# Token stages of a two-block metaformer: centring and variance as 64x64 tiles, hidden banks read in pairs

## The chip, the cores and the metric

The kernel runs on one core of one Trainium2 chip. The metric is the device time of one execution in microseconds (us). The core has the matmul engine (TensorE, PE in the profile), VectorE (DVE), ScalarE (ACT), GpSimd (POOL) and SyncE (SP), which issues the DMAs. Each of them works through its own queue in order and waits on semaphores.

## The reference, cut to what matters

The input is four images of 48 channels and 128x128 pixels in float32. Two blocks follow each other, each of a convolution part and a feed-forward part on tokens, where a token is the 48 channels of one pixel:

```
def _ln_t(v, eps=1e-05):
    m = jnp.mean(v, axis=-1, keepdims=True)
    s = jnp.var(v, axis=-1, keepdims=True)
    return (v - m) / jnp.sqrt(s + eps)
x = x + _L0_conv_ref(_ln_c(x), ...)
t = _to_tokens(x)
t = t + _L0_ffn_ref(_ln_t(t), L0_ffn_W1, L0_ffn_b1, L0_ffn_W2, L0_ffn_b2)
x = _from_tokens(t, x)
x = x + _L1_conv_ref(_ln_c(x), ...)
t = _to_tokens(x)
t = t + _L1_ffn_ref(_ln_t(t), ...)
```

A feed-forward part is a normalisation over the 48 channels, a linear layer to 192 hidden values, a bias and a ReLU, and a linear layer back to 48, with values rounded to an 8-bit float before each product and to a 16-bit float after it. `_ln_c` is the same normalisation ahead of a convolution part.

## The kernel before, in words

The program is a row of stages with a barrier between them: `expand`, `gated_conv`, `token_mix` for the first block, `wavelet`, `attention_maps`, `fusion`, and `token_mix` for the second block. The change is in `token_mix` (lines 669 to 1060) alone. It runs twice. I call the runs the first and the second token stage.

A step of a token stage handles 512 pixels of two images at once: image h (0 or 1) lies on partitions 64h to 64h+47. There are 64 steps (32 blocks of pixels, two pairs of images). The pieces of a step's work are:

- `project` (lines 852, 855 in the first stage, 858 in the second): a linear layer of the convolution part; VectorE adds the residual (`add_residual`, lines 1006, 1008, 1011), which gives `x1`.
- `centre_in` (L863): a matmul with a 112x112 matrix that holds `I - 1/48` for each image's 48 channels, so it subtracts the mean. ScalarE squares the result (L926), `variance` (L881) averages the squares by a second 112x112 matmul, ScalarE takes `Ln` (L933) and `Exp` (L936) for the reciprocal root, and VectorE multiplies (`quantize_norm`, L1019), which gives the 8-bit `xq`.
- `hide(m)` (L894), m = 0, 1: two matmuls, one for each image, 96 hidden values each. ScalarE rounds each of the four results to 16 bits (`round_hidden(m)`, L943, which reads one bank of 512 columns at a time), VectorE adds bias and ReLU for each m (L1025) and casts all to 8 bits (`quantize_hidden`, L1033).
- `show` (L906): four matmuls that sum into `x2_bank`; ScalarE rounds (`round_shown`, L949), VectorE adds bias and residual (`add_shown`, L1039, L1044), and the result `x2` is stored.
- In the first stage alone, a second normalisation of `x2` for the following convolution: `centre_out` (L869), a square (L926), `variance("out")` (L881), `Ln` and `Exp`, `normalise` (L1053), and a store.

PSUM has eight banks. The first stage uses four for centring, two for `x1_bank` (projection and variance of `x1`) and `x2_bank` (`show` and variance of `x2`), and two for the hidden values. So there `hide(1)` writes over the banks of `hide(0)` and waits for ScalarE's copies (`h16_ready`). The second stage has four hidden banks and no such wait.

The order on each engine is written out by a list of pairs (stage, piece), which `staged` walks: in turn k, a piece with stage s works on step k - s. In the first stage PE's list is

```
pieces = [(0, project), (3, show), (2, hide(0)), (4, centre_out), (2, hide(1)), (1, variance("in")), (5, variance("out")), (0, centre_in)]
```

and ScalarE's list is

```
pieces = [(3, round_shown), (2, round_hidden(0)), (4, square("out")), (2, round_hidden(1)), (1, root("in")), (5, root("out")), (0, square("in"))]
```

VectorE's list is `add_residual`, `add_shown`, `bias_hidden`, `quantize_hidden`, `quantize_norm`, `normalise`. `project` waits until `Ln` of step k-2 has read `x1_bank`. `show` waits for `hq` (L1033) and, in the first stage, for `Ln` of the variance that shares `x2_bank` with it.

## Time and profile before

| | |
|---|---|
| runs, median of 3 | 2696.87 us (2694.13 to 2699.63) |
| profiled execution, its own time | 2706.45 us |
| span of its trace | 2704.7 us |
| TensorE busy | 2289.2 us (85%) |
| VectorE busy | 1528.8 us (57%) |
| ScalarE busy | 1125.6 us (42%) |
| granted TensorE clock, mean | 0.923 of full |

The span runs from the first to the last instruction; the execution's own time is 1.75 us longer. A matmul in float32 stands in the trace as two records, so 64 centrings of a stage are x128. The length of a record holds a tail after its last column, so records that follow each other without a gap overlap. PEclk is the granted TensorE clock: 1.00 is 2.4 GHz and 0.50 is 1.2 GHz, the only two levels in this trace.

### The profile page before, as it was taken

How to read it: one execution, taken by the hardware profiler on the slowest of the kernel's cores; microseconds unless marked ns; L12 is line 12 of the kernel's file. 1: busy time of each engine (PE TensorE's matmuls, PEld its weight loads, DVE VectorE, ACT ScalarE, POOL GpSimd, SP SyncE). 2: the span in 40 equal slices, each digit the busy share in tenths (PEclk: the TensorE clock that was granted, in tenths of full speed). 3: DMA queues.
4: the chain of work that ended last, by engine and by line, in shares of the span. 5: the costliest groups of instructions: out<-in, count | busy, mean ns of one | idle time of the engine just before them, and what ended most of it. 6: DMA issues, size and time to landing. Idle time of an engine off the chain costs nothing. (4 is left out here: it accounts for less than half of the span.)

```text
span 2704.7 us, 62201 instructions
## 1 busy us (share of the span) xinstructions
PE 2289.2 (85%) x21290; PEld 1246.6 (46%) x21290; DVE 1528.8 (57%) x2692; ACT 1125.6 (42%) x2338; POOL 443.6 (16%) x677
## 2 busy tenths in 40 slices
PE   5677749859998799999869999999975999688887
PEld 2334325647776333333336676666651232233332
DVE  3344421101112577777658888888861455477776
ACT  4344412101111688888723222322210121477776
POOL 7510001510000000000024444444420000000000
PEclk9888857979999899999969999999986899799998
DMA  6987875987773677777556666666636999233332
GB/s 137 260 226 213 230 217 188 311 252 277 272 274 133 125 145 145 150 144 144 109 110 149 149 139 140 146 149 144 138 100 128 237 266 255 76 105 105 105 105 76
DMA packets 533431, 457.77 MB, mean 169 GB/s; under 512 B 316712, under 2 KB 445680, under 8 KB 529970
## 3 DMA queue, kind: packets, MB, share of 16 engines
q1 hardware_dynamic: 462738, 424.85, 61.8%
q0 software_dynamic: 6032, 23.54, 3.4%
q10 hardware_dynamic: 64560, 7.92, 2.2%
q8 instruction: 78, 1.28, 0.2%
q14 instruction: 23, 0.19, 0.0%
HBM read 271.56 MB, written 186.40 MB: 169 GB/s over the span
## 5 line engine op out<-in xcount | busy, mean ns | idle before, releaser
L593 PE MATMUL gate_ps<-gate_data,gate_wt 64*64 64x289 f32 x6144 | 392.1, 412 | 48.3 <-DVE gate_out L654 29.3
L593 PEld LDWEIGHTS gate_ps<-gate_data,gate_wt 64*64 64x64 f32 x6144 | 296.7, 135 | 144.8 <-issue 64.4
L654 DVE TENSOR_TENSOR gate_out<-gate_gelu,gate_ps 128x578 f32<-128x578 f32 x96 | 72.2, 756 | 413.9 <-PE gate_ps L593 342.8
L943 ACT CAST mix_h<-mix_bank 96x512 f16<-96x512 f32 x512 | 267.6, 593 | 6.3 <-PE mix_bank L894 2.5
L1600 POOL TENSOR_TENSOR wav_diag<-wav_eye,wav_coefs 128x256 f32<-128x256 f32 x96 | 77.4, 827 | 885.8 <-DVE wav_up_cols L1680 816.3
L631 ACT ACTIVATE gate_gelu<-gate_ps 128x578 f32<-128x578 f32 x96 | 62.7, 653 | 372.0 <-PE gate_ps L593 321.8
L2020 PE MATMUL fus_bank<-fus_xt,fus_taps 76*32 76x512 f32 x1344 | 164.0, 641 | 29.0 <-DMA fus_shift<-gate_shift 24.6
L286 DVE COPY exp_out<-exp_y 128x384 f32<-128x384 f32 x192 | 102.8, 567 | 150.6 <-PE exp_y L249 148.9
L1025 DVE TENSOR_SCALAR mix_hb<-mix_h,mix_b1q 96x1024 f16<-96x1024 f16 x256 | 122.7, 479 | 93.6 <-ACT mix_h L943 93.6
L894 PE MATMUL mix_bank<-mix_xq,mix_w1q 112*96 112x512 fp8e5 x512 | 143.5, 382 | 29.1 <-ACT mix_h L943 23.0
L1033 DVE CAST mix_hq<-mix_hb 96x2048 fp8e5<-96x2048 f16 x128 | 156.5, 1223 | 19.5 <-DVE mix_hb L1025 16.4
L906 PE MATMUL mix_x_bank<-mix_hq,mix_w2q 96*112 96x512 fp8e5 x512 | 137.6, 392 | 29.9 <-DVE mix_hq L1033 27.7
L230 PE MATMUL exp_c<-exp_xt,exp_center 112*112 112x512 f32 x128 | 82.2, 755 | 72.2 <-DMA exp_xt<-in_x_dram 71.7
L1466 PE MATMUL wav_full_bank<-wav_halves,wav_base_w 80*32 80x256 f32 x2304 | 138.0, 386 | 0.0
L863 PE MATMUL mix_centre_in<-mix_x,mix_center 112*112 112x512 f32 x256 | 134.6, 608 | 2.1 <-DVE mix_x L1008 1.2
L949 ACT CAST mix_y<-mix_x_bank 112x512 f16<-112x512 f32 x128 | 74.9, 585 | 143.6 <-PE mix_x_bank L906 143.6
L881 PE MATMUL mix_x_bank<-mix_sq_in,mix_average 112*112 112x512 f32 x256 | 132.9, 601 | 2.1 <-DVE mix_x L1008 1.2
L249 PE MATMUL exp_y<-exp_win,exp_xb 48*128 48x192 f32 x1024 | 112.4, 353 | 13.4 <-ACT exp_out L286 5.9
L858 PE MATMUL mix_x_bank<-mix_sc,mix_proj 112*112 112x512 f32 x128 | 72.8, 651 | 58.2 <-ACT mix_logv_in L933 37.1
L1407 PE MATMUL wav_front<-wav_strips,wav_front_w 48*32 48x256 f32 x3840 | 118.2, 385 | 0.0
L1607 POOL TENSOR_TENSOR wav_pool<-wav_scaled,wav_diag 128x256 f32<-128x256 f32 x96 | 67.9, 728 | 277.0 <-ACT wav_scaled L1523 277.0
L249 PEld LDWEIGHTS exp_y<-exp_win,exp_xb 48*128 48x128 f32 x1024 | 86.9, 195 | 54.4 <-issue 34.2
(227 smaller groups left out, 4016.2 us busy)
## 6 DMA issues: line engine op xcount, KB each, us to landing
y<-exp_out SPq DMA_DIRECT2D x64, 816.0 KB, 12.2
gate_data<-y SPq DMA_DIRECT2D x24, 2176.0 KB
g<-gate_out SPq DMA_DIRECT2D x48, 578.0 KB, 4.4
mix_sc<-g SPq DMA_DIRECT2D x31, 816.0 KB
gate_wt<-wm SPq DMA_DIRECT2D x96, 256.0 KB, 8.8
wav_strips<-xp SPq DMA_DIRECT2D x96, 204.0 KB, 3.9
wav_halves<-xp SPq DMA_DIRECT2D x48, 340.0 KB
init<-wav_init SPq DMA_DIRECT2D x48, 268.0 KB, 2.4
```

The lines of the kernel that those rows point to most:

```text
L249: mm = pe.matmul(ps_y[h][q % 2][:, O2 * x:O2 * (x + 1)], xb[u][rows, 2 * q + x].rearrange("c s y x -> c (s y x)"), win[rows, :], start=Tru ...
L593: mm = pe.matmul(banks(a, v)[64 * g:64 * (g + 1), r], wt[q][64 * r:64 * (r + 1), 2 * a + g, n, :], src, start=n == 0, stop=n == 3)
L863: pe.matmul(centre_bank["in"][at.pair][0:CP, :], center[:, :], x1[at.slot][:, :], start=True, stop=True).then_inc(centered["in"], 1)
L881: pe.matmul(var_bank[v][0:CP, :], average[:, :], sq[v][at.pair][:, :], start=True, stop=True).then_inc(var[v], 1)
L894: pe.matmul(bank[(2 * m + h) % len(bank)][0:HID, :], w1q[:, h, m, :], xq[at.pair][:, :], start=True, stop=True).then_inc(hidden, 1)
L906: mm = pe.matmul(x2_bank[0:CP, :], w2q[:, h, m, :], hq[at.pair][:, m, h, :], start=(h + m == 0), stop=(h + m == 2))
L943: act.copy(h16[at.pair][:, m, h, :], bank[(2 * m + h) % len(bank)][0:HID, :]).then_inc(h16_ready, 1)
L1025: relu = dve.tensor_scalar(hb[at.pair][:, m, :, :].rearrange("p h n -> p (h n)"), h16[at.pair][:, m, :, :].rearrange("p h n -> p (h n)"), ...
L1033: dve.tensor_copy(hq[at.pair][:, :, :, :].rearrange("p m h n -> p (m h n)"), hb[at.pair][:, :, :, :].rearrange("p m h n -> p (m h n)"), sa ...
L1407: x = pe.matmul(half(u, r, 0, Q0)[STRIP * g:STRIP * (g + 1)], front_w[u][64 * r:64 * r + K0, 2 + dx, :], strips[u][64 * r:64 * r + K0, g, ...
L1466: x = pe.matmul(images(full_bank[u][STRIP * g:STRIP * (g + 1), :])[:, :, e::2], base_w[u][:, e, dx, :], halves[u][:, g, :, 1 + dx:1 + dx + ...
L2020: mm = pe.matmul(bank[u][0][STRIP * s:STRIP * (s + 1), :], taps[u][0:K2, dx, :], xt[u][:, s, :, dx:dx + W], start=dx == 0, stop=dx == TAPS ...
```

## The change

Centring becomes two matmuls of one image each, and they exchange the images: image 0, on partitions 0 to 47, is written to partitions 64 to 111, and image 1 to partitions 0 to 63 (with zero columns of weights, so that all rows of the tile are written). The variance becomes two matmuls that stay on their partitions. So the four matmuls of a variance and a centring use four different 64x64 tiles of the engine. The weights of `hide` and the rows that `store_norm` reads are swapped to match. In PE's list of the first stage `centre_out` moves behind `hide(1)` and `variance("out")`; `variance("in")` and `centre_in` then stand next to each other. ScalarE's list is the same. The hidden banks become pairs of two banks (one pair in the first stage, two in the second), each read by one copy of 1024 columns; a semaphore is raised once for a pair. One memset of 16 columns is added ahead of a stage.

```diff
@@ -716,7 +716,7 @@
-        bank = [k.ps(f"bank{j}") for j in range(8 - 2 - 2 * len(norms))]
+        pairs = [k.ps(f"bank{j}", (128, 2 * NT)) for j in range(3 - len(norms))]
@@ -812,7 +812,7 @@
-                        rows = slice(PADH * h, PADH * h + C)
+                        rows = slice(PADH * (1 - h), PADH * (1 - h) + C)
@@ -858,16 +858,20 @@
+                def exchange(v, at, x):
+                    pe.sem_inc(pe_turn, 1)
+                    pe.matmul(centre_bank[v][at.pair][PADH:CP, :], center[0:C, 0:C], x[0:C, :], start=True, stop=True)
+                    pe.matmul(centre_bank[v][at.pair][0:PADH, :], center[PADH:CP, PADH:128], x[PADH:CP, :],
+                              start=True, stop=True).then_inc(centered[v], 1)
+
                 def centre_in(at):
                     pe.wait_ge(x1_ready, at.n + 1)
-                    pe.matmul(centre_bank["in"][at.pair][0:CP, :], center[:, :], x1[at.slot][:, :],
-                              start=True, stop=True).then_inc(centered["in"], 1)
+                    exchange("in", at, x1[at.slot])
...
@@ -878,7 +882,9 @@
-                        pe.matmul(var_bank[v][0:CP, :], average[:, :], sq[v][at.pair][:, :],
+                        pe.sem_inc(pe_turn, 1)
+                        pe.matmul(var_bank[v][0:PADH, :], average[0:C, 0:PADH], sq[v][at.pair][0:C, :], start=True, stop=True)
+                        pe.matmul(var_bank[v][PADH:CP, :], average[PADH:CP, PADH:CP], sq[v][at.pair][PADH:CP, :],
                                   start=True, stop=True).then_inc(var[v], 1)
@@ -887,12 +893,13 @@
                         pe.wait_ge(xq_ready, at.n + 1)
-                        if m == 1 and len(bank) == 2:
-                            pe.wait_ge(h16_ready, 4 * at.n + 2)
+                        if m == 1 and len(pairs) == 1:
+                            pe.wait_ge(h16_ready, 2 * at.n + 1)
                         pe.sem_inc(pe_turn, 1)
                         for h in range(2):
-                            pe.matmul(bank[(2 * m + h) % len(bank)][0:HID, :], w1q[:, h, m, :], xq[at.pair][:, :],
-                                      start=True, stop=True).then_inc(hidden, 1)
+                            mm = pe.matmul(pairs[m % len(pairs)][0:HID, NT * h:NT * (h + 1)], w1q[:, 1 - h, m, :],
+                                           xq[at.pair][:, :], start=True, stop=True)
+                        mm.then_inc(hidden, 1)
@@ -909,7 +916,7 @@
-                    pieces = [(0, project), (3, show), (2, hide(0)), (4, centre_out), (2, hide(1)), (1, variance("in")), (5, variance("out")), (0, centre_in)]
+                    pieces = [(0, project), (3, show), (2, hide(0)), (2, hide(1)), (5, variance("out")), (4, centre_out), (1, variance("in")), (0, centre_in)]
@@ -938,10 +945,9 @@
-                        for h in range(2):
-                            act.wait_ge(hidden, 4 * at.n + 2 * m + h + 1)
-                            act.copy(h16[at.pair][:, m, h, :], bank[(2 * m + h) % len(bank)][0:HID, :]
-                                     ).then_inc(h16_ready, 1)
+                        act.wait_ge(hidden, 2 * at.n + m + 1)
+                        act.copy(h16[at.pair][:, m, :, :].rearrange("p h n -> p (h n)"), pairs[m % len(pairs)][0:HID, :]
+                                 ).then_inc(h16_ready, 1)
```

The list moves instructions on PE. In the body of the first token stage's loop one turn of PE reads, before the change (L852 and L855 project, L906 show, L894 hide, L869 centre_out, L881 variance, L863 centre_in):

```order
L852 MATMUL mix_x_bank<-mix_sc,mix_proj 48x448 x2
L855 MATMUL mix_x_bank<-mix_sc,mix_proj 48x64 x2
L906 MATMUL mix_x_bank<-mix_hq,mix_w2q 112x512 x4
L894 MATMUL mix_bank<-mix_xq,mix_w1q 96x512 x2
L869 MATMUL mix_centre_out<-mix_x,mix_center 112x512
L894 MATMUL mix_bank<-mix_xq,mix_w1q 96x512 x2
L881 MATMUL mix_x_bank<-mix_sq_in,mix_average 112x512
L881 MATMUL mix_x_bank<-mix_sq_out,mix_average 112x512
L863 MATMUL mix_centre_in<-mix_x,mix_center 112x512
```

and in the changed kernel (L913 show, L900 hide, L886 and L887 variance, L863 and L864 centring):

```order
L852 MATMUL mix_x_bank<-mix_sc,mix_proj 48x448 x2
L855 MATMUL mix_x_bank<-mix_sc,mix_proj 48x64 x2
L913 MATMUL mix_x_bank<-mix_hq,mix_w2q 112x512 x4
L900 MATMUL mix_bank<-mix_xq,mix_w1q 96x512 x4
L886 MATMUL mix_x_bank<-mix_sq_out,mix_average 64x512
L887 MATMUL mix_x_bank<-mix_sq_out,mix_average 48x512
L863 MATMUL mix_centre_out<-mix_x,mix_center 48x512
L864 MATMUL mix_centre_out<-mix_x,mix_center 64x512
L886 MATMUL mix_x_bank<-mix_sq_in,mix_average 64x512
L887 MATMUL mix_x_bank<-mix_sq_in,mix_average 48x512
L863 MATMUL mix_centre_in<-mix_x,mix_center 48x512
L864 MATMUL mix_centre_in<-mix_x,mix_center 64x512
```

The four hide matmuls now follow each other, and centre_out stands behind them and behind the variance of `x2`.

The same turn on ScalarE in the changed kernel (L955 round_shown, L949 round_hidden, L933 square, L940 Ln, L943 Exp):

```order
L955 CAST mix_y<-mix_x_bank 112x512
L949 CAST mix_h<-mix_bank 96x1024
L933 ACTIVATE mix_sq_out<-mix_centre_out 112x512
L949 CAST mix_h<-mix_bank 96x1024
L940 ACTIVATE mix_logv_in<-mix_x_bank,mix_eps 112x512
L943 ACTIVATE mix_rstd_in<-mix_logv_in 112x512
L940 ACTIVATE mix_logv_out<-mix_x_bank,mix_eps 112x512
L943 ACTIVATE mix_rstd_out<-mix_logv_out 112x512
L933 ACTIVATE mix_sq_in<-mix_centre_in 112x512
```

Before, it is the same row of pieces, with two copies of 512 columns where one of 1024 stands now; the square of centre_out keeps its place between the two reads of hidden values.

## Rows read from the trace of the kernel before

**Rows 1.** The page: granted TensorE clock in 40 slices of the span, tenths of full.

```profile
PEclk9888857979999899999969999999986899799998
```

**Rows 2.** Both stages: length, PE, PEld, DVE, ACT, POOL busy, PEclk, DMA share, GB/s.

```profile
872.00:1360.00 488.00, 428.17 (x1536) 174.76 (x1536) 354.14 (x594) 394.06 (x705) 0.00 (x0) 0.95 0.70 134
...
2312.00:2705.00 393.00, 310.34 (x896) 123.93 (x896) 286.25 (x468) 271.74 (x513) 0.00 (x0) 0.95 0.35 97
```

**Rows 3.** Line 949 (one copy a step) in each stage: duration, first and last start.

```profile
L949 ACT CAST mix_y<-mix_x_bank x64: 585/585/586, 906.0 to 1344.9; 112x512 f16<-112x512 f32 x64
...
L949 ACT CAST mix_y<-mix_x_bank x64: 585/585/586, 2342.3 to 2699.5; 112x512 f16<-112x512 f32 x64
```

**Rows 4.** Timeline of one step of the first stage: start us, us, engine, line, [idle before].

```profile
1106.55 1.07 PE L906 MATMUL mix_x_bank<-mix_hq,mix_w2q 96*112 96x512 fp8e5 x4
...
1107.45 0.60 PE L894 MATMUL mix_bank<-mix_xq,mix_w1q 112*96 112x512 fp8e5 x2
1107.65 0.59 ACT L949 CAST mix_y<-mix_x_bank 112x512 f16<-112x512 f32 x1 [1.09 <-PE mix_x_bank L906]
...
1108.14 1.07 ACT L943 CAST mix_h<-mix_bank 96x512 f16<-96x512 f32 x2
...
1109.09 0.62 ACT L926 ACTIVATE mix_sq_out<-mix_centre_out 112x512 f32<-112x512 f32 x1
...
1109.35 0.60 PE L894 MATMUL mix_bank<-mix_xq,mix_w1q 112*96 112x512 fp8e5 x2 [0.44 <-ACT mix_h L943]
...
1110.88 0.48 DVE L1025 TENSOR_SCALAR mix_hb<-mix_h,mix_b1q 96x1024 f16<-96x1024 f16 x1 [0.95 <-ACT mix_h L943]
...
1111.51 1.02 PE L863 MATMUL mix_centre_in<-mix_x,mix_center 112*112 112x512 f32 x2
...
1111.51 1.22 DVE L1033 CAST mix_hq<-mix_hb 96x2048 fp8e5<-96x2048 f16 x1 [0.15 <-DVE mix_hb L1025]
...
1112.46 0.97 PE L852 MATMUL mix_x_bank<-mix_sc,mix_proj 96*48 96x448 f32 x4
...
1113.48 0.42 PE L906 MATMUL mix_x_bank<-mix_hq,mix_w2q 96*112 96x512 fp8e5 x1
```

**Rows 5.** Timeline of one step of the second stage, the same columns.

```profile
2504.80 1.04 PE L906 MATMUL mix_x_bank<-mix_hq,mix_w2q 96*112 96x512 fp8e5 x4 [0.30 <-DVE mix_hq L1033]
...
2506.36 2.04 ACT L943 CAST mix_h<-mix_bank 96x512 f16<-96x512 f32 x4
...
2508.26 0.72 ACT L933 ACTIVATE mix_logv_in<-mix_x_bank,mix_eps 112x512 f32<-112x512 f32 x1
...
2509.07 1.22 DVE L1033 CAST mix_hq<-mix_hb 96x2048 fp8e5<-96x2048 f16 x1 [0.15 <-DVE mix_hb L1025]
...
2510.44 0.39 PE L906 MATMUL mix_x_bank<-mix_hq,mix_w2q 96*112 96x512 fp8e5 x1 [0.29 <-DVE mix_hq L1033]
```

**Rows 6.** Groups of like instructions: count, busy us, mean ns, idle before.

```profile
L943 ACT CAST mix_h<-mix_bank 96x512 f16<-96x512 f32 x512 | 267.6, 593 | 6.3 <-PE mix_bank L894 2.5
...
L621 ACT ACTIVATE gate_stage<-gate_ps,gate_cg_b 96x1024 f32<-96x1024 f32 x10 | 10.7, 1105 | 14.0 <-PE gate_ps L565 14.0
...
L613 ACT ACTIVATE gate_hid<-gate_ps,gate_cg_b 128x512 f32<-128x512 f32 x2 | 1.4, 688 | 13.2 <-PE gate_ps L555 13.2
```

**Rows 7.** The page's group of the 64x64 tile matmuls in `gated_conv`.

```profile
L593 PE MATMUL gate_ps<-gate_data,gate_wt 64*64 64x289 f32 x6144 | 392.1, 412 | 48.3 <-DVE gate_out L654 29.3
```

**Rows 8.** Busy time and granted clock in four short stretches, columns as in rows 2.

```profile
489.30:496.10 6.80, 3.09 (x52) 2.27 (x48) 1.43 (x2) 1.30 (x2) 0.39 (x2) 1.00 1.01 316
...
1337.80:1342.60 4.80, 2.70 (x8) 0.79 (x6) 2.96 (x6) 4.39 (x8) 0.00 (x0) 1.00 0.35 82
1342.70:1356.80 14.10, 10.79 (x14) 3.42 (x14) 3.12 (x6) 4.41 (x7) 0.00 (x0) 0.50 0.20 44
889.70:898.90 9.20, 7.89 (x16) 2.42 (x18) 1.54 (x4) 2.09 (x4) 0.00 (x0) 0.50 0.82 134
```

**Rows 9.** Timeline in the last steps of the first stage, at half clock.

```profile
1342.94 1.92 PE L906 MATMUL mix_x_bank<-mix_hq,mix_w2q 96*112 96x512 fp8e5 x4 [2.07 <-DVE mix_hq L1033]
```

More of the change, by code:

```diff
@@ L680, in token_mix @@
         k = Bench(nc, st, tag)
-        center, average = k.sb("center", [CP, CP]), k.sb("average", [CP, CP])
+        center, average = k.sb("center", [CP, 128]), k.sb("average", [CP, CP])
         eps = k.sb("eps", [128, 2])
@@ L754, in _ @@
                 sp.wait_ge(prepared, 1)
-                sp.dma_start(center[:, :], const(t, "center")[0:CP]).then_inc(weights_in, 16)
+                sp.dma_start(center[:, 0:CP], const(t, "center")[0:CP]).then_inc(weights_in, 16)
                 sp.dma_start(average[:, :], const(t, "average")[0:CP]).then_inc(weights_in, 16)
@@ L868, in centre_out @@
                     pe.wait_ge(xn_ready, at.n + 1)
-                    pe.matmul(centre_bank["out"][at.pair][0:CP, :], center[:, :], x2[at.pair][:, :],
-                              start=True, stop=True).then_inc(centered["out"], 1)
+                    exchange("out", at, x2[at.pair])
                 def variance(v):
@@ L960, in _ @@
                 dve.memset(eps[:, 1:2], 1e-6)
+                dve.memset(center[:, CP:128], 0.0)
                 dve.memset(w1q[:, :, :, :], 0.0)
@@ L1023, in bias_hidden @@
                     for m in range(2):
-                        dve.wait_ge(h16_ready, 4 * at.n + 2 * m + 2)
+                        dve.wait_ge(h16_ready, 2 * at.n + m + 1)
                         relu = dve.tensor_scalar(hb[at.pair][:, m, :, :].rearrange("p h n -> p (h n)"),
```

## The prediction

> **What bounds the kernel now.** I read the slices first, then the windows of the two token stages, since only they are touched, then one step of each in the timeline. The stages take about 488 and 393 of 2704.7 us, mostly at full clock [rows 1, 2]. The last and the first of 64 copies of `x2_bank` (63 steps) lie 438.9 us apart in the first stage and 357.2 us in the second [rows 3]: 6.97 and 5.67 us a step.
>
> In the first stage PE sets the pace. `show` starts at 1106.55 and again at 1113.48 [rows 4], 6.93 us later, and PE's records fill all of it but 0.44 us, which is `hide(1)` waiting for ScalarE to read the hidden banks [rows 4]. VectorE's cast L1033 ended at 1111.51 + 1.22 = 1112.73, so `show` did not wait for it. The rest of the mean of 6.97 is steps a little late for data.
>
> In the second stage PE waits. The step is 2510.44 - 2504.80 = 5.64 us, and `show` waits for the cast L1033, idle 0.29 us [rows 5]. The loop runs from `show` through L949, four copies of hidden values (2.04 us), the bias and the cast on VectorE, and back to `show`. PE is not what ends last there.
>
> **The copies.** Two copies of 512 columns become one of 1024. No cast of 1024 columns is in the trace. Bounds: two copies one behind the other take 1.07 us [rows 4]; the ScalarE operation L621 with 1024 columns takes 1105 ns and L613 with 512 takes 688 [rows 6], a difference of 417 ns, so 593 + 417 = 1010 ns. I take 1.01. The saving is 0.06 us a copy on the wait, 0.11 us for the two pairs of a step. In the second stage they are on the loop: 5.64 - 0.11 = 5.53, times 61 full steps, **-7 us**. At the other bound it is nothing.
>
> **The tiles.** A centring is two records of 0.86 us together before the next starts, with a tail of 0.17 us behind (1.02 us in all) [rows 4]. Four different tiles at once are in the trace: 6144 records of 289 columns took 392.1 us [rows 7], 0.064 us each, while a record of 512 columns takes 0.43 us, 0.24 for 289: 3.8 abreast. So a variance with its centring costs 0.43 x 8 / 3.8 = 0.9 us instead of 1.72. The other end is no overlap beyond two, 1.72. I take 0.88, as rows 7 have the same tile. PE saves 2 x 0.84 us a step in the first stage and 0.84 in the second, where it only lengthens PE's wait.
>
> The engine changes its tiling at the ends of each group. From L863 (112*112, last column at 1111.51 + 0.86 = 1112.37) to L852 (96*48) at 1112.46 such a change costs 0.09 us [rows 4]; I add 0.09 once to the loop below. The Trainium skill, "TensorEngine Tiling (Array Packing)", Key Properties, says that a change of tiling mode drains the engine. Waiting for the whole tail instead would be 0.17 in place of 0.09, 5 us over the first stage.
>
> **The order in the first stage.** ScalarE still has the square of `centre_out` between its two reads of hidden values. PE now issues `centre_out` behind `hide(1)`, and `hide(1)` waits for ScalarE's first read. Before, `centre_out` ran while that read went on. Now the pieces form one loop, counted from a `show` [rows 4]:
>
> - `show` 0 to 1.07; ScalarE's L949 at 1.10; the pair copy 0.49 later (1107.65 to 1108.14), 1.59 to 2.60.
> - `hide(1)` 0.14 after the copy (1109.21 to 1109.35), at 2.74; its two matmuls take 0.44: 3.18; change of tiling: 3.27; variance and centring abreast 0.88 + tail 0.17: 4.32.
> - Square at 4.36, 0.53 until ScalarE can start the next (0.62 less 0.09): 4.89; second pair copy to 5.90.
> - VectorE's bias at 5.93, 0.48, pause 0.15, cast 1.22: 7.78; next `show` 0.15 later (2510.29 to 2510.44, a loop that waits in the same way) [rows 5]: **7.93**.
>
> It is 1.0 us longer than the step now, though PE's own work falls to 0.90 (`show`) + 0.88 (`hide`) + 1.76 (two groups) + 1.02 (`project`) = 4.6 us. Against the mean: 63 x (7.93 - 6.97) = **+60 us**. Behind the second copy only ScalarE's logarithms are queued, and `project` waits for the first of them: it starts at 6.5 and ends before 7.6, so it is not last.
>
> **The clock.** In a step of 7.93 us PE idles 1.2 us ahead of `hide(1)`, 1.3 us ahead of `project` and 0.3 us ahead of `show`. The trace has such steps: in the tail of the first stage `project` drops out, and PE was busy 2.70 of 4.80 us at 1337.8 [rows 8]. Then the granted clock fell from 1.00 (2.4 GHz) to 0.50 (1.2 GHz), and it stayed there for 14.10 us in which PE was busy 10.79, 77% [rows 8]. At the stage's start PE was busy 7.89 of 9.20 us (86%), and the clock rose [rows 8]. In the new steps the second half (from 4.5 us on) has PE busy 1.9 of 3.4 us, like the stretch before the fall. Against it stands 3.09 busy of 6.80 us at 489.3 at a clock that stayed 1.00 [rows 8]; but there four full 64x64 tiles worked abreast. I take the fall, since the row of this very stage is the nearest.
>
> At half clock `show` takes 1.92 us instead of 1.07 [rows 9]: the streaming part doubles and the tail stays. So `hide(0)` ends at 2.78, its copy at 3.83, `hide(1)` takes 3.97 to 4.84, the two groups of 1.76 us end at 8.45 and 0.2 later with their tail, the logarithm (0.72, [rows 5]) at 9.4, `project` (1.02 now, 1.78 then) at 11.2, and the next `show` starts at 11.3. The loop over the cast is 10.5. PE is busy about 8.8 of 11.3 us, 78%: nearer to the stretch that stayed low than to the one that rose. I take 85 of 100 steps low: 0.85 x 11.3 + 0.15 x 7.93 = 10.8 us, 63 x (10.8 - 6.97) = **+241 us**, which holds the +60. Ends: half the steps low, mean 9.6, +166; all low, +273.
>
> In the second stage the clock can fall too: 5.53 us with PE busy 4.0, and from the end of the last group to `show` busy 1.1 of 2.7. At half clock PE's sum (show, hide, group) ends at 5.4 us, logarithm 6.1, `project` 7.9: about 8.0 a step. But there PE is then busy almost throughout and the clock rises again soon, as at the start. With 5 of 61 steps low: 5 x 2.5 = +12, with the copies +5. Ends: -7 and a quarter low, +31.
>
> The extra memset (16 columns) and the swapped store rows cost nothing: the weights' loads ahead of a stage hide the memset, and the stores have the same count and size; uncovered, the memset would cost less than a tenth of a us in each stage.
>
> **Sum.** 2706.45 + 241 + 5 = 2952 for the profiled execution, which lies 9.6 us over the median of the runs: **2943**. Its own range: 2706 + 166 - 7 - 10 = 2855 to 2706 + 273 + 31 - 10 = 3000.
>
> **The rivals.**
>
> - **The clock holds** in both stages. Then +60 - 7: 2706 + 53 - 10 = 2750. For it speaks that no idle stretch is over 1.3 us; against it the fall at 1342.6. The Trainium skill, "TensorE: Matmul & The Clock Gate", "Why this matters for your kernels", asks for no long gap between bursts of matmuls; no gap here is long by it, and by that rule this case's 2750 would come out. The trace disagrees so far: the tail fell with PE more than half busy. Chance 0.22.
> - **The tiles do not run four abreast** but two. Then a group takes 1.72, the loop 7.93 + 0.84 = 8.8, PE is busy 6.3 of it and the clock holds: 63 x 1.83 - 7 = +108, 2805. Rows 7 speak against it; for it, that the matrices come from different tensors. Chance 0.06.
> - **Faster**: ScalarE's queue, not the loop, sets the pace: 6.12 us busy of 6.9, less 0.11, with little idle, 6.2 a step: 63 x -0.77 - 7 = -56, 2641. It decides for this if the centred bank is there when the first copy ends, 2.6 us after `show`; by the order it comes 1.7 us later, because `centre_out` stands behind the matmuls that wait for that very copy. Chance 0.03.
> - **No change**: loop and saving cancel. It needs a loop of 7.0, a us less than summed. Chance 0.02.
>
> **How the numbers follow.** The forecast has 0.67. Predicted is its time, 2943. The range reaches down to the held clock, 2745, and up to 2990, leaving out the two cases that are not slower (0.05) and the top, where nearly every step is low (0.1). A measurement of this kernel can tell 0.2% (5 us) from no change. Faster 0.03, same 0.02, slower 0.95.
>
> **What would show it.** In the changed trace: the square of `centre_out` (L933) released by PE L864 with ScalarE idle about 1.7 us before it in each step; the pair copy near 1.01 us; the first of four tile records and the last within one record's length; the copy L955 every 7.9 us where the granted clock is 1.00 and about 11.3 where it is 0.50; 0.50 over most of the first stage. A steady first stage at 1.00 would make it the first rival; a step under 7 us would refute the loop.

## The result, and the profile after

The changed kernel takes 2975.97 us (median of 4 runs, 2974.03 to 2984.54), the kernel before 2695.96 us beside it (4 runs, 2694.13 to 2699.63). The ratio is 1.1043, with an interval of 1.1018 to 1.1068: slower by 10%. The profiled execution took 2984.54 us with a span of 2982.6 us, 277.9 us more than the span before, and its mean granted clock was 0.807.

The page of the changed kernel: the clock slices (which answer to [rows 1]), PE's busy time, the pair copy (to [rows 6]) and the four tile matmuls (count, busy us, mean ns, idle before).

```profile
PEclk9888769899985555555555899999998799799998
...
PE 2434.3 (82%) x22058; PEld 1259.0 (42%) x22058; DVE 1541.1 (52%) x2694; ACT 1118.1 (37%) x2082; POOL 440.4 (15%) x677
...
L949 ACT CAST mix_h<-mix_bank 96x1024 f16<-96x1024 f32 x256 | 251.4, 1008 | 26.6 <-PE mix_bank L900 26.6
...
L886 PE MATMUL mix_x_bank<-mix_sq_in,mix_average 48*64 48x512 f32 x256 | 192.7, 844 | 2.3 <-DVE mix_x L1015 1.3
L863 PE MATMUL mix_centre_in<-mix_x,mix_center 48*48 48x512 f32 x256 | 192.4, 843 | 2.3 <-DVE mix_x L1015 1.3
L864 PE MATMUL mix_centre_in<-mix_x,mix_center 48*64 48x512 f32 x256 | 193.4, 847 | 0.0
L887 PE MATMUL mix_x_bank<-mix_sq_in,mix_average 48*48 48x512 f32 x256 | 191.7, 840 | 0.0
```

Ten slices in a row read 5; in [rows 1] the slices of that stage read 8 and 9, and 6 at its end. PE is busy for 145 us more than before, although the tiles were to save it work. At half clock the columns take twice as long: in the step shown below the next record of a tile starts 0.85 us after the last one (L887 at 1216.26 and 1217.11), in a step at 1.00 of the kernel with repeated work, further down, 0.42 us after it (L891 at 1203.07 and 1203.49).

The copy L955, one in each step, in the two token stages of the changed kernel (they answer to [rows 3]): duration, then first and last start.

```profile
L955 ACT CAST mix_y<-mix_x_bank x64: 586/587/587, 908.1 to 1611.0; 112x512 f16<-112x512 f32 x64
...
L955 ACT CAST mix_y<-mix_x_bank x64: 586/586/587, 2612.0 to 2977.4; 112x512 f16<-112x512 f32 x64
```

First stage: 702.9 us where it was 438.9, so +264.0; 11.16 us a step. Second stage: 365.5 where it was 357.2, +8.3. The work ahead of the first stage, between the stages and at the end makes up the other 5.6 us. So the first stage holds 95% of the loss.

Windows of the changed kernel's first stage, columns as in [rows 2]:

```profile
870.20:1388.90 518.70, 414.80 (x1412) 126.08 (x1412) 246.18 (x412) 263.52 (x387) 0.00 (x0) 0.50 0.48 90
1389.00:1399.00 10.00, 6.20 (x44) 2.24 (x40) 6.96 (x11) 7.76 (x12) 0.00 (x0) 1.00 0.24 48
1400.00:1566.00 166.00, 137.30 (x471) 41.48 (x469) 80.83 (x132) 88.11 (x131) 0.00 (x0) 0.50 0.50 93
```

The clock is at 1.2 GHz from the start of the stage to 1388.9, at 2.4 GHz for 10 us, and low again. Before, it was low at the start as well, but rose at 898.9 and stayed up until 1342.6. So there is no long stretch at full clock that the new loop ends. The clock is low before the first step, and it stays low but for two stretches of 10 us (the other one ends at 1576.7).

Timeline of one low-clock step of the changed kernel (answers to [rows 4]; start us, us, engine, line, [idle before]):

```profile
1210.38 1.96 PE L913 MATMUL mix_x_bank<-mix_hq,mix_w2q 96*112 96x512 fp8e5 x4
...
1212.37 0.59 ACT L955 CAST mix_y<-mix_x_bank 112x512 f16<-112x512 f32 x1 [1.54 <-PE mix_x_bank L913]
...
1213.23 1.01 ACT L949 CAST mix_h<-mix_bank 96x1024 f16<-96x1024 f32 x1 [0.27 <-PE mix_bank L900]
...
1214.38 1.06 PE L900 MATMUL mix_bank<-mix_xq,mix_w1q 112*96 112x512 fp8e5 x2 [1.19 <-ACT mix_h L949]
...
1215.37 1.11 PE L886 MATMUL mix_x_bank<-mix_sq_out,mix_average 48*64 48x512 f32 x1
...
1215.37 1.09 PE L887 MATMUL mix_x_bank<-mix_sq_out,mix_average 48*48 48x512 f32 x1
...
1215.38 1.09 PE L863 MATMUL mix_centre_out<-mix_x,mix_center 48*48 48x512 f32 x1
...
1215.39 1.11 PE L864 MATMUL mix_centre_out<-mix_x,mix_center 48*64 48x512 f32 x1
...
1217.45 0.60 ACT L933 ACTIVATE mix_sq_out<-mix_centre_out 112x512 f32<-112x512 f32 x1 [3.21 <-PE mix_centre_out L864]
1217.94 1.00 ACT L949 CAST mix_h<-mix_bank 96x1024 f16<-96x1024 f32 x1
...
1219.10 0.69 ACT L940 ACTIVATE mix_logv_in<-mix_x_bank,mix_eps 112x512 f32<-112x512 f32 x1 [0.16 <-PE mix_x_bank L887]
...
1219.61 1.22 DVE L1040 CAST mix_hq<-mix_hb 96x2048 fp8e5<-96x2048 f16 x1 [0.15 <-DVE mix_hb L1032]
...
1219.84 1.74 PE L852 MATMUL mix_x_bank<-mix_sc,mix_proj 96*48 96x448 f32 x4 [0.78 <-ACT mix_logv_in L940]
...
1221.71 1.96 PE L913 MATMUL mix_x_bank<-mix_hq,mix_w2q 96*112 96x512 fp8e5 x4
```

The four tiles start within 0.02 us of each other: they run four abreast. `hide(1)` waits 1.19 us for the first pair copy, `centre_out` stands behind it, and ScalarE idles 3.21 us for it ahead of the second pair copy. These are the links of the prediction's loop. At half clock, though, they do not set the step: the cast L1040 ends at 1219.61 + 1.22 = 1220.83, and `show` starts at 1221.71, right behind `project`, which has waited 0.78 us for the logarithm behind the two groups of tiles. The 1221.71 - 1210.38 = 11.33 us of the step run from `show` over the first pair copy, `hide(1)`, the two groups, the logarithm and `project`. The prediction has that chain for half clock; its logarithm ends 9.41 us after `show`, for 9.4 predicted. The waits of the stage (engine and line, what for, us in total, times, longest), of which the last two are those of PE, which sets the pace:

```profile
DVE mix_hb L1032 <- ACT mix_h L949: 264.5, 98, 4.2
ACT mix_sq_out L933 <- PE mix_centre_out L864: 192.7, 61, 3.2
...
PE mix_bank L900 <- ACT mix_h L949: 61.9, 52, 1.2
...
PE mix_x_bank L852 <- ACT mix_logv_in L940: 49.7, 62, 1.4
```

So far the times and the links of the prediction are there. Whether idle time in the new order is what kept the clock low is what the experiments had to say.

### The profile page after: what moved, and what is told of

The parts are those of the page before. It is cut to its first block and busy times, and to the rows that moved or that the text cites. A ratio compares the mean times of both kernels' runs of the same rounds, so it can differ in the third digit from the quotient of the medians.

```text
span 2982.6 us, 63453 instructions
## 1 busy us (share of the span) xinstructions
PE 2434.3 (82%) x22058; PEld 1259.0 (42%) x22058; DVE 1541.1 (52%) x2694; ACT 1118.1 (37%) x2082; POOL 440.4 (15%) x677
## 5 line engine op out<-in xcount | busy, mean ns | idle before, releaser
L593 PEld LDWEIGHTS gate_ps<-gate_data,gate_wt 64*64 64x64 f32 x6144 | 329.2, 135 | 113.8 <-issue 65.9
L900 PE MATMUL mix_bank<-mix_xq,mix_w1q 112*96 112x512 fp8e5 x512 | 213.6, 534 | 75.7 <-ACT mix_h L949 61.9
L949 ACT CAST mix_h<-mix_bank 96x1024 f16<-96x1024 f32 x256 | 251.4, 1008 | 26.6 <-PE mix_bank L900 26.6
L913 PE MATMUL mix_x_bank<-mix_hq,mix_w2q 96*112 96x512 fp8e5 x512 | 199.8, 532 | 34.2 <-DVE mix_hq L1040 28.6
L886 PE MATMUL mix_x_bank<-mix_sq_in,mix_average 48*64 48x512 f32 x256 | 192.7, 844 | 2.3 <-DVE mix_x L1015 1.3
L863 PE MATMUL mix_centre_in<-mix_x,mix_center 48*48 48x512 f32 x256 | 192.4, 843 | 2.3 <-DVE mix_x L1015 1.3
L864 PE MATMUL mix_centre_in<-mix_x,mix_center 48*64 48x512 f32 x256 | 193.4, 847 | 0.0
L887 PE MATMUL mix_x_bank<-mix_sq_in,mix_average 48*48 48x512 f32 x256 | 191.7, 840 | 0.0
L1040 DVE CAST mix_hq<-mix_hb 96x2048 fp8e5<-96x2048 f16 x128 | 156.6, 1223 | 21.2 <-DVE mix_hb L1032 19.1
L852 PE MATMUL mix_x_bank<-mix_sc,mix_proj 96*48 96x448 f32 x256 | 108.0, 941 | 69.2 <-ACT mix_logv_in L940 49.7
L900 PEld LDWEIGHTS mix_bank<-mix_xq,mix_w1q 112*96 112x96 fp8e5 x512 | 76.9, 164 | 186.9 <-issue 168.6
L955 ACT CAST mix_y<-mix_x_bank 112x512 f16<-112x512 f32 x128 | 75.1, 586 | 199.7 <-PE mix_x_bank L913 199.7
```

The lines of the kernel that those rows point to most:

```text
L593: mm = pe.matmul(banks(a, v)[64 * g:64 * (g + 1), r], wt[q][64 * r:64 * (r + 1), 2 * a + g, n, :], src, start=n == 0, stop=n == 3)
L863: pe.matmul(centre_bank[v][at.pair][PADH:CP, :], center[0:C, 0:C], x[0:C, :], start=True, stop=True)
L864: pe.matmul(centre_bank[v][at.pair][0:PADH, :], center[PADH:CP, PADH:128], x[PADH:CP, :], start=True, stop=True).then_inc(centered[v], 1)
L886: pe.matmul(var_bank[v][0:PADH, :], average[0:C, 0:PADH], sq[v][at.pair][0:C, :], start=True, stop=True)
L887: pe.matmul(var_bank[v][PADH:CP, :], average[PADH:CP, PADH:CP], sq[v][at.pair][PADH:CP, :], start=True, stop=True).then_inc(var[v], 1)
L900: mm = pe.matmul(pairs[m % len(pairs)][0:HID, NT * h:NT * (h + 1)], w1q[:, 1 - h, m, :], xq[at.pair][:, :], start=True, stop=True)
```

## The experiments

"Before" in each batch is the kernel before, run beside it: 2701.21 us in the first, 2689.32 in the second, 2702.10 in the third. The first stage's length is that from the first to the last copy of `x2_bank`, as in [rows 3], over 63 steps.

In the expectations theory A is the prediction's: the moved order makes PE idle, and that holds the clock down.

### First batch: the order, the tiles, and more work

**Undo the move.** The changed kernel with PE's old list:

```diff
-pieces = [(0, project), (3, show), (2, hide(0)), (2, hide(1)), (5, variance("out")), (4, centre_out), (1, variance("in")), (0, centre_in)]
+pieces = [(0, project), (3, show), (2, hide(0)), (4, centre_out), (2, hide(1)), (1, variance("in")), (5, variance("out")), (0, centre_in)]
```

> The change with PE's old list: centre_out again between hide(0) and hide(1); tiles and pair copies stay. Theory A (the moved centring makes a loop of 7.9 us, and its idle time brings the low clock): the first stage steps in 6.4 us at full clock, 25 to 35 us less than before the change, the second stage stays as in the changed kernel (about +8), total 2670 us (2655 to 2690). Theory B (the tiles alone leave PE too idle, wherever centre_out stands): granted clock 0.50 over most of the first stage, steps of about 11 us, total over 2900.

Measured: 2965.98 us (2958.29 to 2977.29), ratio 1.0993 [1.0937, 1.1049]. The order gone, nearly the whole loss stays. The window of its first stage:

```profile
890.00:1600.00 710.00, 700.97 (x2008) 195.50 (x2008) 359.16 (x568) 397.88 (x566) 0.00 (x0) 0.50 0.47 88
```

and one of its steps on PE:

```profile
1210.73 1.73 PE L852 MATMUL mix_x_bank<-mix_sc,mix_proj 96*48 96x448 f32 x4
...
1212.61 1.96 PE L913 MATMUL mix_x_bank<-mix_hq,mix_w2q 96*112 96x512 fp8e5 x4
1214.36 1.06 PE L900 MATMUL mix_bank<-mix_xq,mix_w1q 112*96 112x512 fp8e5 x2
1215.35 1.09 PE L863 MATMUL mix_centre_out<-mix_x,mix_center 48*48 48x512 f32 x1
...
1217.25 1.09 PE L900 MATMUL mix_bank<-mix_xq,mix_w1q 112*96 112x512 fp8e5 x2
1218.27 1.11 PE L886 MATMUL mix_x_bank<-mix_sq_in,mix_average 48*64 48x512 f32 x1
...
1221.87 0.99 PE L852 MATMUL mix_x_bank<-mix_sc,mix_proj 96*48 96x448 f32 x2
```

PE is busy 701 of 710 us, 99%, and the clock is 0.50 all the time. A step takes 1221.87 - 1210.73 = 11.14 us, set by PE alone. Theory A is refuted for these tiles: the clock stays low with PE almost never idle. Theory B has the outcome, but its reason (the tiles leave PE too idle) falls by the same 99%. The run also shows what the move costs at this clock: 11.33 - 11.14 = 0.2 us a step.

**The order alone.** The kernel before (whole 112x112 matmuls, single banks) with the changed list, the reverse of the diff above.

> The kernel before with the new PE list of the first stage alone: whole 112x112 centring and variance, banks read one by one. Theory A: the loop is longer by the move, 8.8 us a step at full clock (centre_out now ends two whole matmuls behind hide(1)), with PE busier than in the changed kernel, so the clock mostly holds: first stage about +120 to +170 us, total 2815 to 2870. Theory B: the order is harmless without the tiles, total within 20 us of 2696.

Measured: 2844.36 us (2833.97 to 2855.09), ratio 1.0542 [1.0484, 1.06], as expected. The first stage takes 587.7 us, 8.75 us a step where the clock is 1.00 and 10.45 where it dips (its mean from 930 to 1480 is 0.93). ScalarE's wait for `centre_out` is there with whole matmuls too:

```profile
ACT mix_sq_out L926 <- PE mix_centre_out L869: 183.0, 59, 4.6
```

So the loop of the prediction is real, and the order costs about 150 us in this stage by itself: 8.75 - 6.93 = 1.8 us a step at full clock, and the rest in the steps where the clock dips; in the kernel before it stays up from 898.9 to 1342.6.

**The tiles alone.** The kernel before with the tiles, the old list and one copy for each bank. The lines below differ from the changed kernel, whose list is taken back as well.

```diff
-        pairs = [k.ps(f"bank{j}", (128, 2 * NT)) for j in range(3 - len(norms))]
+        bank = [k.ps(f"bank{j}") for j in range(8 - 2 - 2 * len(norms))]
...
-                        act.wait_ge(hidden, 2 * at.n + m + 1)
-                        act.copy(h16[at.pair][:, m, :, :].rearrange("p h n -> p (h n)"), pairs[m % len(pairs)][0:HID, :]
+                        for h in range(2):
+                            act.wait_ge(hidden, 4 * at.n + 2 * m + h + 1)
+                            act.copy(h16[at.pair][:, m, h, :], bank[(2 * m + h) % len(bank)][0:HID, :]
```

> Tiles alone: old PE list, hidden banks read one by one. Theory A: first stage 6.4 us a step as with undo_move (the pair copies are worth 0.1 us or nothing there), second stage 5.64 at full clock but with PE idle more and the clock low now and then, +8 to +12 us against before; total 2680 (2665 to 2695). Theory B: over 2900.

Measured: 2973.78 us (2958.65 to 2996.69), ratio 1.0994 [1.0939, 1.105]; 11.14 us a step, and the first stage takes 695.0 us:

```profile
930.00:1600.00 670.00, 668.14 (x1916) 185.50 (x1910) 336.10 (x539) 380.22 (x662) 0.00 (x0) 0.50 0.47 89
```

The tiles by themselves bring all of it.

**More work.** The changed kernel with the centring of `x1` in the first stage issued three times over; the repeats write the same values.

```diff
+                    for _ in range(2 if wide and v == "in" else 0):
+                        pe.matmul(centre_bank[v][at.pair][PADH:CP, :], center[0:C, 0:C], x[0:C, :], start=True, stop=True)
+                        pe.matmul(centre_bank[v][at.pair][0:PADH, :], center[PADH:CP, PADH:128], x[PADH:CP, :],
+                                  start=True, stop=True)
```

> The changed kernel with the centring of x1 in the first stage computed three times over instead of once (the same result; 3.5 us more TensorE time a step at half clock). Theory A: at full clock the repeats fill the idle time ahead of project, the loop over hide(1) and centre_out stays 7.9 us, the clock holds at 1.00 for most of the stage, and the stage takes about 500 us instead of 703: total 2770 to 2800, faster than the changed kernel though it does more. Rival C (the low clock is not a matter of PE's idle time): clock stays 0.50, the repeats lengthen the step to about 14 us, total over 3120.

Measured: 2784.11 us (2778.31 to 2801.7), ratio 1.0321 [1.026, 1.0382]. With 512 more matmul records it is 192 us faster than the changed kernel. The first stage takes 505.2 us, and in a window of it the clock is up:

```profile
930.00:1400.00 470.00, 392.83 (x2348) 141.74 (x2349) 314.65 (x527) 346.20 (x529) 0.00 (x0) 1.00 0.66 125
```

Its step on ScalarE:

```profile
1200.42 0.59 ACT L959 CAST mix_y<-mix_x_bank 112x512 f16<-112x512 f32 x1 [0.18 <-PE mix_x_bank L917]
1200.90 1.01 ACT L953 CAST mix_h<-mix_bank 96x1024 f16<-96x1024 f32 x1
1203.77 0.60 ACT L937 ACTIVATE mix_sq_out<-mix_centre_out 112x512 f32<-112x512 f32 x1 [1.86 <-PE mix_centre_out L868]
...
1208.43 0.59 ACT L959 CAST mix_y<-mix_x_bank 112x512 f16<-112x512 f32 x1 [0.18 <-PE mix_x_bank L917]
```

From one copy to the next 8.01 us pass, and the idle time before the square, 1.86 us, stands in it. The total lies in theory A's range, and rival C is out. But the run does not separate idle time from work done: the repeats fill the one and add to the other. By itself it would have seemed to confirm the theory that the run without the move refutes.

### Second batch: what holds the clock down

PE's idle time being ruled out as what holds the clock down with these tiles, two things were left: how many of the array's rows the tiles fill, and that a low clock might keep itself, because it stretches the step. The tiles read 48 rows each, 96 of 128 together. The whole matmul reads 112.

**64 rows in one tile.** PE's old list, and the first of the two matmuls of a centring and of a variance reads 16 more rows, which are zeros:

```diff
-pe.matmul(centre_bank[v][at.pair][PADH:CP, :], center[0:C, 0:C], x[0:C, :], start=True, stop=True)
+pe.matmul(centre_bank[v][at.pair][PADH:CP, :], center[0:PADH, 0:C], x[0:PADH, :], start=True, stop=True)
...
-pe.matmul(var_bank[v][0:PADH, :], average[0:C, 0:PADH], sq[v][at.pair][0:C, :], start=True, stop=True)
+pe.matmul(var_bank[v][0:PADH, :], average[0:PADH, 0:PADH], sq[v][at.pair][0:PADH, :], start=True, stop=True)
```

> undo_move with 64 instead of 48 rows in the first matmul of each centring and variance (16 more rows of zeros; the durations of the matmuls are the same). If the clock depends on how many rows of the array the matmuls fill: it rises in the first steps as in the kernel before, steps are 6.4 us, the first stage takes about 405 us instead of 439, total 2665 to 2685. If rows do not matter and only the time that PE is busy does: as undo_move, 11.14 us a step and about 2966.

Measured: 2716.3 us (2709.13 to 2718.56), ratio 1.0085 [1.0044, 1.0126]. Its first stage in a window:

```profile
930.00:1340.00 410.00, 352.15 (x1868) 117.64 (x1867) 317.85 (x524) 354.13 (x526) 0.00 (x0) 0.99 0.75 143
```

and the wait of `project` among the waits of the same stretch:

```profile
PE mix_x_bank L852 <- DMA mix_sc<-g: 33.4, 27, 2.7
```

Sixteen rows of zeros bring 250 us (2965.98 to 2716.3). That rows matter is confirmed. The gain over the kernel before, which was expected too, is missing: 27 steps of this stretch wait for the load of the projection's input, 33.4 us together. The stage takes 444.5 us, nearly the 438.9 of before.

**The same with the new list.**

> The changed kernel with the 64 rows and PE's new list. Theory A with rows counted: full clock in about two thirds of the first stage, steps of 7.9 us there and 9 to 11.4 between, first stage about 555 us, total 2820 to 2870. If rows do not matter: as the changed kernel, 2976.

Measured: 2849.99 us (2842.34 to 2851.51), ratio 1.0581 [1.0538, 1.0623], as expected. That is 126 us better than the changed kernel. Steps take 8.0 us at full clock and 9 to 11.4 where it is low, and it changes often. The window, and the start of one `show` at full clock:

```profile
930.00:1470.00 540.00, 380.01 (x1897) 125.33 (x1894) 322.10 (x533) 355.08 (x538) 0.00 (x0) 0.81 0.58 109
...
1205.56 1.04 PE L913 MATMUL mix_x_bank<-mix_hq,mix_w2q 96*112 96x512 fp8e5 x4 [0.35 <-DVE mix_hq L1040]
```

Here `show` waits for the cast, so the loop of the prediction sets the 8.0 us: this is the moved order's own price with the tiles at full clock. And the order moves the clock too, once the rows are there: with the same tiles the old list had PE busy for 86% of its window and the clock at 0.99, the new list 70% and 0.81.

**A start at full clock.** The changed kernel with PE's old list, tiles of 48 rows, and the centring of `x1` three times over (the same values again) in the first 12 steps alone, which are written out ahead of the loop. The loop's body is that of the kernel whose clock never rose.

```diff
+                    for _ in range(2 if wide and v == "in" and isinstance(at.n, int) and at.n < LEAD else 0):
...
```

> undo_move (tiles, pair copies, PE's old list) with the centring of x1 computed three times over in the first 12 steps of the first stage alone, which are written out ahead of the loop; the loop's body is that of undo_move to the instruction. Theory D (the body has two states that feed themselves: at half clock PE works without a pause and the clock still stays low, at full clock the same body would keep it high; the stage starts low and never leaves): the clock rises within the first steps, as it did in filler, and holds for some of the stage; steps of 6.4 to 6.5 us there; total 2665 to 2800 depending on how long it holds. Theory E (the tiles of 48 rows pull the clock down from any start): it falls back to 0.50 within 50 us of the repeats' end and steps are 11.14 us again, total over 2930.

Measured: 2716.69, 2925.86, 2910.19 and 2862.54 us. The profile is that of the first:

```profile
896.90:1347.00 450.10, 389.78 (x2102) 132.06 (x2100) 344.85 (x568) 383.00 (x567) 0.00 (x0) 1.00 0.73 138
```

In this execution the same loop body stayed at 1.00 to the end of the stage, with steps from 6.55 to 8.0 us, where it took 11.14 us at 0.50 without the start. So the body can run either way for a whole stage, and here the start made the difference. In this one execution theory D held. The three others lie outside the ranges of both theories; their mean granted clock was 0.82 to 0.85 against 0.917. They have no trace, so where they lost the clock isn't known, and how well this body keeps a high clock is open.

**A version to beat both.** Tiles with 64 rows in the first stage (old list), whole matmuls in the second stage with pairs.

> First stage as in rows64_old_list; second stage with the whole 112x112 matmuls of the kernel before and the pair copies. Expected faster than both kernels: first stage 405 us (-34), second stage 5.53 us a step with the clock steady (-7): total 2655 (2645 to 2670).

Measured: 2706.01 us (2695.88 to 2723.23), ratio 1.0058 [1.0006, 1.011]. The second stage gained as expected (351.6 us for 357.2). The first took 448.7 us, with the same wait for the load among its waits from 930 to 1340, and with the clock low now and then:

```profile
PE mix_x_bank L852 <- DMA mix_sc<-g: 32.4, 26, 2.5
```

A miss: it is no faster than the kernel before.

### Third batch: the loads, ScalarE's order, the pairs

**Pairs alone.** The kernel before with the paired banks, whole matmuls, and the old list.

> The kernel before with the pair copies alone. Second stage 5.53 us a step at steady full clock, -7 us; first stage unchanged within 3 us (PE sets the pace there). Total 2685 to 2692 where the kernel before is 2696. If the pair copies had cost the first stage its time (rival: hide(1) waits longer for one read of 1024 columns), the total would be over 2700.

Measured: 2691.8 us (12 runs, 2679.77 to 2709.52), ratio 0.9975 [0.995, 1.0]. In its trace the second stage takes 349.7 us for 357.2, -7.5, and the first 436.9 for 438.9. The traced execution is the fastest of the 12, and the interval of the whole reaches 1, so the total does not show the gain; the steps do (5.52 us for 5.64).

**The load one step earlier.** 64 rows, the old list, and `mix_sc<-g` issued a step earlier in SyncE's queue, ahead of the stores. It becomes a piece of its own, `fetch_sc` (its body and its first issue, ahead of the loop, are not shown):

```diff
-                def load(at):
+                def fetch_sc(at):
...
-                staged(sp, 2 * N, SLOTS, [(0, load), (4, store_x2)] + [(7, store_norm)] * wide, LEAD)
+                staged(sp, 2 * N, SLOTS, [(0, load)] + [(-1, fetch_sc)] * wide + [(4, store_x2)] + [(7, store_norm)] * wide, LEAD)
```

> rows64_old_list with the load of the projection's input for the next step issued one step earlier, ahead of that step's stores in SyncE's queue. Theory F (in rows64_old_list the first stage waits for that load in every other step, so the tiles' gain is capped by it): every step is near 6.55 us, first stage about -25 us, total 2690 (2680 to 2700). If the load's own transfer rate is the limit: unchanged, 2716.

Measured: 2686.54 us (2674.82 to 2702.63), ratio 0.9949 [0.9925, 0.9974]. Successive steps on PE:

```profile
1099.78 1.04 PE L921 MATMUL mix_x_bank<-mix_hq,mix_w2q 96*112 96x512 fp8e5 x4 [0.34 <-ACT mix_logv_out L948]
...
1106.33 1.04 PE L921 MATMUL mix_x_bank<-mix_hq,mix_w2q 96*112 96x512 fp8e5 x4 [0.35 <-ACT mix_logv_out L948]
```

Nearly every step takes 6.55 us, and the first stage 417.2. Once the load is early, the wait for data is gone, and ScalarE's `Ln` is what `show` waits for.

**ScalarE's order with the new list.** 64 rows, the changed list, and the square of `centre_out` behind both copies:

```diff
-pieces = [(3, round_shown), (2, round_hidden(0)), (4, square("out")), (2, round_hidden(1)), (1, root("in")), (5, root("out")), (0, square("in"))]
+pieces = [(3, round_shown), (2, round_hidden(0)), (2, round_hidden(1)), (4, square("out")), (1, root("in")), (5, root("out")), (0, square("in"))]
```

> rows64_new_list with ScalarE's square of centre_out behind its second read of hidden values, so that the loop over hide(1) and centre_out is cut while PE's list stays the new one. Theory A: the step at full clock falls from 8.0 to 7.3 us (now bound by show, hide(1), variance, centring, square, logarithms), the clock holds longer, total 2740 to 2780 against 2850. If the moved square is not what closes the loop: 2850.

Measured: 2771.43 us (2759.02 to 2787.06), ratio 1.0242 [1.0197, 1.0288], as expected; 7.41 us a step at full clock for 8.0, and the clock is higher than with the square in its old place (0.92 for 0.81). The window, and a step of ScalarE:

```profile
930.00:1400.00 470.00, 327.52 (x1864) 111.96 (x1865) 320.89 (x528) 359.17 (x529) 0.00 (x0) 0.92 0.66 124
...
1203.34 1.01 ACT L949 CAST mix_h<-mix_bank 96x1024 f16<-96x1024 f32 x1
1205.14 1.01 ACT L949 CAST mix_h<-mix_bank 96x1024 f16<-96x1024 f32 x1 [0.79 <-PE mix_bank L900]
1206.21 0.60 ACT L933 ACTIVATE mix_sq_out<-mix_centre_out 112x512 f32<-112x512 f32 x1
```

The second copy no longer waits for `centre_out`, only for `hide(1)`. The 0.6 us that this gives back is the link in the loop that the prediction named. The rest of the distance to 6.55 stays: in this step `hide(1)` still waits 1.24 us for the first copy, with no matmul to fill the wait.

**The parts that work.** 64 rows, the old list, pairs, the early load, the repeats in the first five steps of the first stage; whole matmuls and pairs in the second.

> 64-row tiles with PE's old list, pair copies and the early load in the first stage, the centring of x1 three times over in its first five steps (so that the clock rises early), whole matmuls and pair copies in the second stage. Expected: first stage 6.55 us a step, -25 us against before, second stage -7: total 2660 (2650 to 2680), faster than both kernels.

Measured: 2670.25 us (6 runs, 2663.7 to 2681.97), ratio 0.9888 [0.9854, 0.9922]. It beats the kernel before by 1.1%, clear of the interval, and the changed one by 306 us. Its first stage takes 413.2 us (25.7 less than before), its second 352.4 (4.8 less), and the clock holds:

```profile
930.00:1310.00 380.00, 345.40 (x1844) 115.91 (x1843) 311.44 (x521) 351.16 (x523) 0.00 (x0) 1.00 0.80 153
```

## Why the prediction was right, and where its reason was wrong

The time, 2976, lies 33 us over the forecast of 2943 and in its own range. Point by point:

- **The loop over the moved `centre_out`**: predicted 7.93 us a step at full clock. Measured 8.0 with 64 rows, where `show` waits for the cast, and 8.01 with the repeated centring. The release (L933 by PE L864) and the idle time (1.7 us predicted, 1.86 measured) are there. Putting ScalarE's square behind the copy shortened the step by 0.6 us, which shows the link by intervention.
- **The step at half clock**: 11.3 predicted, 11.33 measured, by the chain over `project` that the prediction gives for it. PE is busy 414.80 of 518.70 us there, 80%, for 78.
- **How many steps are low**: 85 of 100 assumed. Between 870.12 and 1641.5 the clock was up for two stretches of 10 us only: +264 us in place of +241. This share is the term that was mis-sized, and most of the 33 us.
- **The tiles**: four abreast, as taken from [rows 7], starts within 0.02 us. The rival with two abreast is out.
- **The pair copy**: 1.01 predicted, 1.008 measured; -7.5 us in the second stage of the kernel with pairs alone, for -7. The two other kernels with pairs and whole matmuls there have -5.6 and -4.8.
- **The second stage**: +5 predicted, +8.3 measured. Steps take 5.52 us (5.53 predicted) at 1.00 and 5.9 to 6.6 us where the clock dips. Against the kernel with pairs alone (349.7 us), the tiles cost 15.8 us there. The fall is not one stretch of 5 steps, as the prediction had it, but many short ones.
- **Why the clock is low**: this step failed, though its outcome held, so that the time came out near is in part luck. The prediction put it that in the new steps "the second half (from 4.5 us on) has PE busy 1.9 of 3.4 us, like the stretch before the fall", so idle time that the move makes would bring the clock down. In the trace no such fall begins the low stretch: the clock was low from before the first step, and the only two falls in the stage end stretches of 10 us. With the move undone, PE was busy 99% of the stage, at 0.50 throughout, and the kernel gained only 10 us. The tiles alone, without move and pairs, cost the same. What decides here is in the tiles: 16 more rows in one of them, zeros all, took 250 us off with the old list and 126 us with the new. And the start matters: one loop body ran at 6.55 to 8.0 us for a stage in one execution and at 11.14 us without the repeats ahead of it. Idle time is not nothing: with 64 rows the new list had 0.81 where the old one had 0.99. But with tiles of 48 rows taking it away did not bring the clock back. The prediction's comparison "PE is busy about 8.8 of 11.3 us, 78%: nearer to the stretch that stayed low than to the one that rose" drew on busy time, which does not tell these cases apart: 99% busy stayed low here. Its own row of full 64x64 tiles at 1.00 with PE busy 3.09 of 6.80 us, set aside as the farther one, pointed at the rows.

The Trainium skill, "TensorE: Matmul & The Clock Gate", "Why this matters for your kernels", by which a dense stream without long gaps runs at the high clock, was one of the rivals, with 2750 us. The kernel with the move undone is the plainest case against it in these runs: no gaps, and 0.50 for the whole stage. Where the clock did hold, the changed list gave 2784 us (with the repeats in it), so that rival's price was near.

So the loss divides otherwise than the prediction's words suggest. The tiles of 48 rows cost it by the clock, with either list; the move costs next to nothing beside that, and shows its own 60 us and more only when the clock is up (with 64 rows 134 us, 2849.99 - 2716.3). The two do not add.

What stays open: what decides how long the clock stays up when the start is the same (only times and mean clocks of the other executions are known), and why rows count: the edit made one of the two tiles a full one of 64 rows, so the number of rows and the full tile are not told apart. That rows matter is shown for these two shapes in this stage alone. An order of PE between the two lists wasn't tried.

## What to carry to other kernels

Before counting time saved by packing small matmuls into tiles, look at the granted clock of that stage, and ask what the tiles leave of the array's rows: here a cheaper matmul made the stage 1.6 times as long, and rows of zeros gave it back. When an instruction is moved behind a wait, look where its consumer stands in the other engine's queue; if it stands between two things that the wait is about, the three make a loop. And when the engine that set the pace gets faster, look for the load that was just in time behind it, and issue it earlier.

## What the runs showed of the hardware

- A matmul engine that works almost without a pause can stay at 1.2 GHz for over 700 us: 700.97 busy of 710.00 us at 0.50, with tiles that read 48 rows. With 64 rows in one of two tiles the same order had 0.99.
- One loop body ran at 11.14 us a step at 0.50 for a whole stage, and in one execution, after a start with more matmuls, at 6.55 to 8.0 us at 1.00 for 450 us. Three more executions of that kernel took 2862.54 to 2925.86 us for 2716.69.
- With tiles of 64 and 48 rows the order alone moved the clock: 0.99 with PE busy 352.15 of 410.00 us, 0.81 with 380.01 of 540.00.
- 512 more matmul records made the changed kernel 192 us faster (2976 to 2784).
- A variance and a centring as four tiles take 0.90 us at full clock (a group starts at 1202.59 and the next at 1203.49 in the kernel with the repeats), about what one whole matmul takes by itself (0.86 us [rows 4]).
